# Two buffers instead of three in the layer norm, and two slabs of Wo issued before the end of attention, in a transformer layer on eight cores

## What is computed

```python
xn = _layernorm(x, axis=-1)
# attention
q = rms_norm(xn @ Wq + bq, gq); k = rms_norm(xn @ Wk + bk, gk); v = xn @ Wv + bv
attn = softmax(einsum('bhqd,bhkd->bhqk', q, k) / sqrt(128))
attention = einsum('bhqk,bhkd->bhqd', attn, v) @ Wo + bo
# mixture block
h = relu(xn @ up_w) ** 2
moe = ((xn @ fc1_w) @ expert_w) * sum(top2(xn @ gate_w))
block = _layernorm(h @ down_w + moe @ fc2_w) * ln_gamma + ln_beta
return x + attention + block
```

## Time and profile before

| What | us |
|---|---|
| Timed runs: median of 2 | 23123.45 |
| lowest and highest | 23106.04 and 23140.86 |
| The profiled execution, its time | 22976.93 |
| its span, slowest core (core 1) | 22975.4 |
| its span, quickest core (core 6) | 21209.9 |
| TensorE busy in the span of core 1 | 18832.4 |
| DVE busy | 5890.9 |
| ACT busy | 3216.8 |
| POOL busy | 1163.6 |

### The profile page before, as it was taken

One profiled execution on the slowest core, in us unless ns is written; L12 is line 12 of the kernel. 1 busy time (PEld: TensorE's weight loads), 2 busy tenths in 40 slices (PEclk: granted clock), 3 DMA queues, 4 the chain that ended last, 5 costly groups with the idle time before them and its releaser, 6 DMA issues.

```text
span 22975.4 us, 184204 instructions; the slowest of 8 cores (21209.9 to 22975.4 us)
## 1 busy us (share of the span) xinstructions
PE 18832.4 (82%) x68608; PEld 6619.9 (29%) x68608; DVE 5890.9 (26%) x8491; ACT 3216.8 (14%) x4933; POOL 1163.6 (5%) x1998
## 2 busy tenths in 40 slices
PE   0299999989997989999999999988799987787830
PEld 0133333333332222222222222123344433333310
DVE  3211001111004554444444554300000000000034
ACT  3100000000001333333333333300000000000001
POOL 0000000000000000000000000000022312000000
PEclk9988888777887887777777777677799998898965
DMA  3522222232211000000000000056577765777753
GB/s 119 136 42 44 44 44 44 46 61 44 41 40 24 17 12 17 12 12 17 12 12 16 12 14 14 3 130 153 138 191 190 195 192 116 155 159 159 156 155 148
DMA packets 2040998, 1799.03 MB, mean 78 GB/s; under 512 B 788165, under 2 KB 1951429, under 8 KB 2023109
## 3 DMA queue, kind: packets, MB, share of 16 engines
q1 hardware_dynamic: 1573354, 1275.24, 20.9%
q0 software_dynamic: 429920, 444.89, 11.5%
q10 hardware_dynamic: 36864, 67.13, 0.9%
HBM read 1778.65 MB, written 302.02 MB: 91 GB/s over the span
## 4 chain that ended last, share of the span: by engine, by line
PE 78%; DMA 8%; DVE 7%; another core or an unknown queue 3%; issue 2%; SPq 1%; ACT 1%; DVEq 0%; POOL 0%; ACTq 0%; POOLq 0%
PE ps L321 24%; PE ps L980 8%; PE ps L781 7%; PE ps L577 7%; PE ps L560 6%; PE ps L575 6%; PE ps L558 5%; PE ps L513 5%; PE ps L700 4%; DMA b<-xnT_sc 3%; DMA b<-x_own 2%; PE ps L985 2%; DVE rowf L585 2%; PE ps L326 1%
## 5 line engine op out<-in xcount | busy, mean ns | idle before, releaser
L321 PE MATMUL ps<-b 128*128 128x512 bf16 x20480 | 5535.0, 439 | 1243.6 <-DMA b<-xn_sc 1098.8
L518 DVE TENSOR_REDUCE mparts<-ps 128x1 f32<-128x512 f32 x4096 | 2826.5, 691 | 3516.9 <-PE ps L513 3442.1
L321 PEld LDWEIGHTS ps<-b 128*128 128x128 bf16 x20480 | 2174.1, 109 | 4408.3 <-issue 4356.0
L565 ACT ACTIVATE b<-ps 128x512 bf16<-128x512 f32 x4096 | 2445.4, 597 | 5510.7 <-PE ps L560 5510.7
L781 PE MATMUL ps<-b 128*128 128x512 bf16 x9920 | 2237.7, 384 | 198.8 <-DMA b<-xnT_sc 130.3
L980 PE MATMUL ps<-b 128*128 128x512 bf16 x8192 | 1810.3, 382 | 635.0 <-DMA b<-fc_w 587.6
L513 PE MATMUL ps<-b 128*128 128x512 bf16 x4096 | 1851.7, 452 | 64.1 <-DVE mparts L518 33.0
L558 PE MATMUL ps<-b 128*128 128x512 bf16 x4096 | 1853.3, 452 | 0.0
L577 PE MATMUL ps<-b 128*128 128x512 bf16 x4096 | 1837.8, 449 | 0.0
L560 PE MATMUL ps<-b,ones_bfr 1*128 1x512 bf16 x4096 | 1814.7, 443 | 0.0
L575 PE MATMUL ps<-b,onescol_bf 128*1 128x512 bf16 x4096 | 1781.4, 435 | 12.2 <-DVE b L602 12.2
(11 more groups left out here) (138 smaller groups left out, 7142.0 us busy)
## 6 DMA issues: line engine op xcount, KB each, us to landing
b<-xnT_sc SPq DMA_DIRECT2D x80, 4096.0 KB, 24.3
b<-x_own SPq DMA_DIRECT2D x32, 2048.0 KB, 14.9
b<-Wk POOLq DMA_DIRECT2D x16, 4096.0 KB, 32.9
b<-Wv POOLq DMA_DIRECT2D x16, 4096.0 KB, 25.9
b<-up_w POOLq DMA_DIRECT2D x16, 4096.0 KB, 53.7
b<-down_w POOLq DMA_DIRECT2D x8, 8192.0 KB, 68.5
b<-moe_sc SPq DMA_DIRECT2D x128, 512.0 KB, 14.7
xn_sc<-b SPq DMA_DIRECT2D x32, 1024.0 KB, 4.7
```

Source lines behind the costliest of these rows:

```text
L321: pe.matmul(ps[bank][:], xnT[:, ch * TOK + tt * 128: ch * TOK + (tt + 1) * 128], wsl[:, ch * 512:(ch + 1) * 512], start=(ch == 0), stop=False)
L518: rr = L.inc(dv.reduce_max(mparts[:, kb:kb + 1], ps[bank][:], axis=AX.X), "dv")
L565: ex = L.inc(ac.activation(PT[kt % 4][:], ps[bank][:], AF.Exp), "ac")
```

## The change

Stage A uses two sets of buffers instead of three: tile i takes set i % 2. The stores use the semaphores `sx0` and `sx1`, and the third set of statistics is gone. The third set's place in `b0` is not used in A, and the others lie closer together.

The slabs of Wo for column blocks 0 and 1 are issued by POOL directly after the loop over heads, ahead of the last `flush_tail`. Two waits are emitted ahead of them, for TensorE's count at the end of B and for the last `sx0` store. `d2_wload` then issues a slab only where it has not been issued, and the bias row always.

```diff
-            rax = [b0f(0, 4096), b0f(4096, 4096), b0f(8192, 4096)]
-            rsq = [b0f(12288, 4096), b0f(16384, 4096), b0f(20480, 4096)]
-            rno = [b0b(49152, 4096), b0b(53248, 4096), b0b(57344, 4096)]
...
+            rax = [b0f(0, 4096), b0f(4096, 4096)]
+            rsq = [b0f(8192, 4096), b0f(12288, 4096)]
+            rno = [b0b(32768, 4096), b0b(36864, 4096)]
...
             for i in range(NT_SEQ):
-                p = i % 3
+                p = i % 2
...
-                SSa = (S, S2, S3)[p]
+                SSa = S if p == 0 else S2
...
-                sxs = ("sx0", "sx1", "sb0")[p]
-                L.wait(ac, "ac", sxs, rno_g[p])
+                L.wait(ac, "ac", f"sx{p}", rno_g[p])
...
+            pe_after_B = L.cnt["pe"]
...
                 d_head_pe[h2] = L.cnt["pe"]
+            wo2 = [b1b(0, 16384), b1b(16384, 16384)]
+            d2_wl = {}
+            L.wait(gd, "gd", "pe", pe_after_B)
+            L.wait(gd, "gd", "sx0", L.cnt["sx0"])
+            for fbp in (0, 1):
+                d2_wl[fbp] = L.inc(gd.dma_start(
+                    out=wo2[fbp % 2].rearrange("p (c f) -> p c f", f=512),
+                    in_=W["Wo"][:, fbp * 512:(fbp + 1) * 512].rearrange(
+                        "(c p) f -> p c f", p=128)), f"w{fbp % 2}", 16)
             flush_tail(*pending)
...
             def d2_wload(fb):
                 if fb >= 8:
                     return
-                L.wait(gd, "gd", "pe", d2_pe.get((fb - 2, NT_OWN - 1), d2_base))
-                d2_wl[fb] = L.inc(gd.dma_start(
...
+                if fb not in d2_wl:
+                    L.wait(gd, "gd", "pe", d2_pe.get((fb - 2, NT_OWN - 1), d2_base))
+                    d2_wl[fb] = L.inc(gd.dma_start(
...
                 L.wait(gd, "gd", "dv", d2_brc.get(fb - 1, 0))
```

More of the change, by code:

```diff
@@ L134, in build @@
                   ("s1", "s2", "mu", "msq", "var", "sd", "rstd", "nbias")}
-        small3 = {nm: sbuf(nm + "_c", [128, 1], F32) for nm in
-                  ("s1", "s2", "mu", "msq", "var", "sd", "rstd", "nbias")}
         mparts = sbuf("mparts", [128, 8], F32)
@@ L140, in build @@
         S2 = small2
-        S3 = small3
         def b0f(lo, n):
@@ L233, in ln_stats @@
                 return stats, sd
-            rax = [b0f(0, 4096), b0f(4096, 4096), b0f(8192, 4096)]
-            rsq = [b0f(12288, 4096), b0f(16384, 4096), b0f(20480, 4096)]
-            rno = [b0b(49152, 4096), b0b(53248, 4096), b0b(57344, 4096)]
-            rax_g = [0, 0, 0]
-            rsq_g = [0, 0, 0]
-            rno_g = [0, 0, 0]
+            rax = [b0f(0, 4096), b0f(4096, 4096)]
+            rsq = [b0f(8192, 4096), b0f(12288, 4096)]
+            rno = [b0b(32768, 4096), b0b(36864, 4096)]
+            rax_g = [0, 0]
+            rsq_g = [0, 0]
+            rno_g = [0, 0]
             for i in range(NT_SEQ):
-                p = i % 3
+                p = i % 2
                 src = x_own if i < NT_OWN else x_oth
@@ L261, in _ @@
                     sy.dma_start(out=xn_sc[i * 128:(i + 1) * 128, :], in_=rno[p]),
-                    sxs, 16)
+                    f"sx{p}", 16)
             if DEBUG_STOP == "A":
@@ L652, in _ @@
                 return finish()
-            wo2 = [b1b(0, 16384), b1b(16384, 16384)]
             ot2 = [b0b(0, 4096), b0b(4096, 4096)]
@@ L660, in _ @@
             d2_st = [0, 0]
-            d2_wl = {}
             d2_brc = {}
@@ L666, in d2_wload @@
                     return
-                L.wait(gd, "gd", "pe", d2_pe.get((fb - 2, NT_OWN - 1), d2_base))
-                d2_wl[fb] = L.inc(gd.dma_start(
-                    out=wo2[fb % 2].rearrange("p (c f) -> p c f", f=512),
-                    in_=W["Wo"][:, fb * 512:(fb + 1) * 512].rearrange(
-                        "(c p) f -> p c f", p=128)), f"w{fb % 2}", 16)
+                if fb not in d2_wl:
+                    L.wait(gd, "gd", "pe", d2_pe.get((fb - 2, NT_OWN - 1), d2_base))
+                    d2_wl[fb] = L.inc(gd.dma_start(
+                        out=wo2[fb % 2].rearrange("p (c f) -> p c f", f=512),
+                        in_=W["Wo"][:, fb * 512:(fb + 1) * 512].rearrange(
+                            "(c p) f -> p c f", p=128)), f"w{fb % 2}", 16)
                 L.wait(gd, "gd", "dv", d2_brc.get(fb - 1, 0))
```

## The result

| | before | changed |
|---|---|---|
| median | 23042.80 us (10 runs) | 23002.14 us (13 runs) |
| lowest to highest | 22681.56 to 23163.19 | 21607.49 to 23175.32 |

The median is 40.7 us lower and lies in the predicted range. That ratio can't be understood without knowing that it takes for each kernel the executions nearest to its own lowest, and that the granted TensorE clock differs from execution to execution: two of the changed kernel's (21607 and 21664 us) had a mean clock of 0.876 or more on every core, and the lowest of the 10 of before took 22681.56 us. So the ratio alone leaves open whether the kernel became faster.

A forecast was written before the change was run, and what follows sets the result against it. The prediction took TensorE and its granted clock to bound the kernel (core 1, 22975.4 us). Stage A 0 plus waits of 28.5 and 6.1 made 34.6 us less, 0.9985 of 23123.45, so 23089 us, range 22970 to 23205.

The forecast's parts named there:

- Stage A costs 0: Layer norm at the start: with two buffers each of the three moved guards waits 0 us, bounds also 0.
- The slabs have landed before the last stores: End of attention: slab 1 lands between 14996 and 15018 us, last stores issue from 15026.57, smallest gap 8 us, cost 0.
- TensorE's first wait: Start of the output projection: idle about 13.5 us instead of 42.0, ended by the `ot_sc` load; 28.5 us gained, bounds 13.9 and 28.8.
- Rival C: Start of the output projection: attention output loads of tiles 0 and 1 take 22.2 us, only 15 us gained, 23108 us; chance 0.13.
- The second wait: Output projection, ahead of tile 2: the wait for the second bias row's cast goes, 6.1 us gained.
- The sum: Whole kernel: 0 for stage A plus 28.5 plus 6.1, 34.6 us less, bounds 15 and 34.9.
- The clock: Granted TensorE clock, whole kernel: widest unknown, 0.001 worth 59 us, +-0.002 giving +-118 us about 23089.
- rival A: Whole kernel: clock outweighs the edit, 0.001 lower gives 23148 us, higher 23030; chance 0.2 slower, 0.1 faster.

The follow-up runs named there:

- The second set of the changed kernel: The changed kernel measured once more without any edit: median 22816.5 us (7 runs), against 22640.5 us (11 runs) of the kernel before in the same hour.

## Why the prediction was right, and where it was wrong

**Stage A costs 0.** Right: the waits sit where they sat, its end is at 818 us in the mean of the cores against 820 and 818 in two profiles of the kernel before, and the kernels with loads ahead show why: SP's queue, not the number of buffers, set the pace.

**The slabs have landed before the last stores.** Right, but with less room than I gave, and by luck in part. I took 35 to 57.2 us for slab 1, the rows of D2 on core 1. It took 56.8 to 63.7 on the eight cores, and the smallest gap was 2.0 us, not 8. Core 1 was the quickest of the eight in the trace of the kernel before: there the same slab took 57.2 to 66.1. The slowest is core 3; the landing of its slabs 0 and 1:

```profile
DMA to landing us min/median/max: 34.7/50.4/66.1
```

The bound was there to read, on another core: 66.1 us against the 65.6 between the issue of slab 1 (14961) and that of the last stores (15026.6). In 66.1 us it would have landed after they were issued.

**TensorE's first wait.** Right in size: 13.65 to 15.12 us on the eight cores of the changed kernel's first profile for the 13.5 forecast, and by the releaser forecast. The 42.02 it came from was that of core 1; the other cores of the kernel before stood 37.4 to 50.1 us. Rival C did not come: the loads of tiles 0 and 1 landed in 7.5 to 12.1 us on the eight cores, not in 22.2. The reading behind the 42 us was half right: the bias row was stuck behind slab 0, but the slab itself, needed just as much, landed 0.1 us earlier. Moving the rows alone would have left the wait as it was, as the kernel with the bias rows first shows.

**The second wait.** Right: 0 to 1.7 us ahead of tile 2, where 6.13 had been on core 1 and 13.89 on core 0.

**The sum.** Right as far as it can be measured: the first wait fell by 28.6 us in the mean of the eight cores (42.7 to 14.1), and a core's span by 26 to 34, with a standard error of 13, for the 34.6 of the sum.

**The clock.** This is the step that failed, the term that set the range. It took "+-0.002 of it is +-118 us", from cores 1 and 3 within one execution, and rival A gave 0.05 to "faster by over 2%", since die 0 would have to come up by 0.008. The spread was too small by far: between executions of one and the same kernel the clock of a die moved from about 0.805 to 0.895, and the time from 21790 to 23163 us. That the ratio came out below the range takes no part of the change: an execution of 21790 us came from the kernel before itself, and of 21357 and 21372 us from the kernels with the bias rows first and with the added matmuls, which hold neither half of it. The change's own gain lies inside the range. The price was too high: cores 1 and 4 of the earlier trace rows differ by 1656.6 us with 0.084 of clock, which is 20 us for 0.001, not 59, so that 2% of the time takes 0.023 of clock and not 0.008. The earlier trace rows already showed both ends side by side, 0.811 and 0.895 in one execution, and I treated the lower one as a property of die 0 and not as a draw.

The trace of the kernel before held more against that. Windows of core 1, then of core 3 on the same die:

```profile
2000.00:2500.00 500.00, 481.97 (x1751) 191.21 (x1750) 55.38 (x97) 11.64 (x20) 8.91 (x8) 0.80 0.25 45
8000.00:8500.00 500.00, 444.56 (x1487) 117.14 (x1487) 275.16 (x403) 171.94 (x288) 19.11 (x36) 0.89 0.06 13
9000.00:9500.00 500.00, 453.81 (x1347) 109.07 (x1346) 245.93 (x362) 155.82 (x261) 17.01 (x32) 0.76 0.06 13
```

```profile
2000.00:2500.00 500.00, 486.18 (x2120) 209.20 (x2118) 46.70 (x68) 0.00 (x0) 8.91 (x8) 0.98 0.26 51
```

On core 1 the clock is 0.89 in one stretch of attention and 0.76 in a later one, with TensorE as busy in both, and at 2000 us the two cores of one die have 0.80 and 0.98. So the low clock comes and goes within an execution, and the 59 us compared two cores that had lost their time in different stages. A range that takes all this in would have reached down to 21300. It would also have said that a comparison by a few executions can come out anywhere within some 6%.

**Whether the change makes the undisturbed clock likelier.** Not shown, and not excluded for good. It first looked so (2 of 14 against 0 of 10). Then the kernel before had such an execution too, and so did three kernels without early slabs. The second set of the changed kernel had none. 4 of 34 and 4 of 65 can't be told apart. No mechanism is in sight either: the clock in the gap and before it is 0.50 with and without the change, and the shorter gap is 27 us of some 22000. The traces speak against one for the early slabs. In the profile after, core 6 is 1224 us behind core 0 at its last store of D (14648.0 and 13423.9) and takes as long as core 0 from there on (7898 and 7894 us): all its loss lies ahead of that place, and the slabs are issued only 69 us before it. In the profile before, core 1 is 1620 us behind core 4 at that place. From the last store of D to the end, 24 of 48 cores with early slabs and 28 of 48 without took less than 8000 us, the others 8025 or more. More executions of both would settle it; there are none. On cores whose clock was not held down there is no trace of the 5%.

## What to carry to other kernels

A third buffer is worth nothing if the load that would fill it is issued in the same queue behind the store of the tile before; look at what stands ahead of the load in its queue before counting buffers, and move the load there (346 us here, with two buffers as well as with three). Transfers that are prefetched on the queue of the previous stage's last stores must land before those are issued, so measure the head start against the slowest such transfer on any core (66.1 us here), and not against the core of the page (57.2). And when the clock moves by a tenth between executions, read a small change at the gap where it acts and on cores at the same clock, not in the quotient of a few whole times.

## What was not expected of the hardware

- In eight-core executions of the same program the mean granted clock of a die lay anywhere from 0.80 to 0.90; 48 executions of the kernel before ranged from 21790 to 23163 us.
- The clock went by pairs of cores and in stretches: in the profile after, from 2000 to 2500 us, cores 4 and 5 had 0.98, and cores 6 and 7 of the same die 0.80 and 0.81; from 16000 to 16500 us it was 0.81 on the first two and 0.92 and 0.93 on the others.
- TensorE at 1.2 GHz (0.50) while it is busy: in the last head, with half of the matmuls of one row or one column, it stayed at 0.50 on both dies in windows in which it was 89% (49.19 of 55 us, core 4) to 97% busy (116.11 of 120 us, core 6 of the changed kernel; on core 1 it was 116.37 of 125). With one more full matmul for each key tile it was 0.91, and the added work made the last head 68 us shorter.
- Small stores on POOL's queue behind two 4 MB slabs: up to 24.9 us instead of 1.7.
